# A one-core GNN and mixture-of-experts kernel: the shared expert's gate and up products between the router and the first routed expert, its down products beside the last one

## What is computed

```
# layer 3 (L3_ffn): shared expert of 768 hidden units
y_shared = jax.nn.silu(t @ Wsg.T) * (t @ Wsu.T) @ Wsd.T
y = (y_routed + y_shared).reshape(b, s, h)
```

## Time and profile before

| | us |
|---|---|
| median of 3 runs | 1854.82 (1854.15 to 1860.57) |
| the profiled execution's own time | 1854.55 |
| its span, first to last instruction | 1852.4 |
| PE busy in it | 1738.4 (94%) |
| `L0_ffn` on PE, about | 540 to 767 |
| expert part of `L3_ffn`, about | 1677 to 1848 |

### The profile page before, as it was taken

The page is one execution under the profiler, slowest core; times in us unless marked ns, Lnnn a source line. Parts: engine busy times, 40 slices in busy tenths (PEclk is TensorE's granted clock), DMA queues, the critical chain, the costliest instruction groups (busy, mean ns, idle before and its releaser), DMA issues.

```text
span 1852.4 us, 27529 instructions
## 1 busy us (share of the span) xinstructions
PE 1738.4 (94%) x12224; PEld 1040.0 (56%) x12224; DVE 624.6 (34%) x1179; ACT 444.2 (24%) x816; POOL 26.7 (1%) x35
## 2 busy tenths in 40 slices
PE   7999899998999999889999988887999999999999
PEld 4675445764456555667654433334575645766566
DVE  4415795038972221361321000002422322234320
ACT  0014684047841110251210000002411010131110
POOL 0000000000000000000000000000002000000000
PEclk9999899999999999989999999999999899999999
DMA  9315875238646877402579999999362154204660
GB/s 375 113 33 188 212 218 207 93 125 220 213 172 239 324 307 284 161 1 103 205 282 389 428 429 429 428 427 428 149 268 102 67 231 194 113 26 153 232 231 18
DMA packets 80749, 408.28 MB, mean 220 GB/s; under 512 B 9768, under 2 KB 50240, under 8 KB 58992
## 3 DMA queue, kind: packets, MB, share of 16 engines
q1 hardware_dynamic: 76112, 402.41, 57.0%
q10 hardware_dynamic: 4512, 4.03, 0.7%
HBM read 400.85 MB, written 5.51 MB: 219 GB/s over the span
## 4 chain that ended last, share of the span: by engine, by line
PE 81%; DMA 12%; DVE 5%; issue 1%; ACT 1%; SPq 0%; POOL 0%; DVEq 0%; ACTq 0%
PE banks L114 79%; DMA weight_ring<-in_L_ffn_c_fc_dram 6%; PE banks L117 2%; DMA weight_ring<-in_L_ffn_c_proj_e_dram 2%; DMA weight_ring<-in_L_gnn_W_in_dram 2%; DVE weight_ring L120 1%; DMA gate_queries<-in_L_gnn_query_rep_dram 1%; DVE stat L266 1%; DVE xn_tok L125 0%; DMA query_parts<-gate_query_parts 0%; DMA ident<-in_c_ident_dram 0%; DVE xT L137 0%; ACT weight_ring L148 0%; DMA node_parts<-gate_node_parts 0%; DVE rgat_xr L137 0%
## 5 line engine op out<-in xcount | busy, mean ns | idle before, releaser
L114 PE MATMUL banks<-weight_ring,xT 128*128 128x384 f32 x864 | 293.5, 492 | 1.5 <-DVE rgat_xr L137 1.5
L120 DVE TENSOR_TENSOR weight_ring<-weight_ring,gate_queries 128x1024 f32<-128x1024 f32 x192 | 223.7, 1221 | 31.6 <-DMA gate_queries<-in_L_gnn_query_rep_dram 15.8
L114 PEld LDWEIGHTS banks<-weight_ring,xT 128*128 128x128 f32 x864 | 162.7, 192 | 109.0 <-issue 8.8
L148 ACT ACTIVATE weight_ring<-banks 128x1024 f32<-128x1024 f32 x192 | 191.0, 1024 | 57.8 <-PE banks L114 54.7
L114 PE MATMUL banks<-xT,weight_ring 128*128 128x256 f32 x792 | 178.7, 380 | 3.2 <-ACT x_tok L151 3.2
L114 PEld LDWEIGHTS banks<-xT,weight_ring 128*128 128x128 f32 x792 | 149.7, 190 | 29.0 <-issue 5.1
L114 PE MATMUL banks<-weight_ring,r_xd 128*32 128x384 f32 (+1 forms) x2304 | 142.7, 406 | 1.1 <-DVE r_xd L124 0.6
L114 PE MATMUL banks<-weight_ring,moe_xdT 128*64 128x384 f32 x720 | 122.0, 489 | 20.6 <-DMA weight_ring<-in_L_ffn_c_fc_dram 19.6
L114 PE MATMUL banks<-weight_ring,selrow 128*32 128x256 f32 x1536 | 104.5, 392 | 12.5 <-DVE weight_ring L120 12.4
L114 PEld LDWEIGHTS banks<-weight_ring,r_xd 128*32 128x32 f32 x2304 | 76.7, 110 | 64.2 <-issue 54.5
L114 PE MATMUL banks<-gate_rows,selrow 96*128 96x512 bf16 x384 | 109.2, 387 | 2.9 <-ACT weight_ring L148 2.2
(11 more groups left out here) (370 smaller groups left out, 1841.8 us busy)
## 6 DMA issues: line engine op xcount, KB each, us to landing
weight_ring<-in_L_ffn_c_fc_dram SPq DMA_DIRECT2D x30, 2304.0 KB, 22.4
weight_ring<-in_L_ffn_c_proj_e_dram SPq DMA_DIRECT2D x21, 2304.0 KB, 28.8
gate_queries<-in_L_gnn_query_rep_dram SPq DMA_DIRECT2D x48, 512.0 KB, 3.9
weight_slot_heads<-in_L_ffn_c_proj_e_dram SPq DMA_DIRECT2D x9, 2304.0 KB, 28.3
weight_ring<-in_L_ffn_w_gate_dram SPq DMA_DIRECT2D x8, 2304.0 KB, 10.0
weight_ring<-in_L_ffn_w_up_dram SPq DMA_DIRECT2D x8, 2304.0 KB, 9.0
weight_ring<-in_L_ffn_w_down_dram SPq DMA_DIRECT2D x8, 2304.0 KB, 9.2
weight_ring<-in_L_ffn_w_dram SPq DMA_DIRECT2D x16, 1152.0 KB, 7.6
```

The source lines that it names most:

```text
L114: return self.e.matmul(out, lhsT, rhs, start=start, stop=stop)
L120: return self.e.tensor_tensor(out, a, b, op)
L148: return self.e.activation(out, a, f, **kw)
```

## The change

In both steps the shared expert's gate and up products move ahead of the first routed expert, and its down products, cut in three, take their places in the two hooks and in `combine_last_pe`; `shared_pe` is gone. In layer 0 the alpha row is spread behind the chunks, and the multiplication of the hidden units with alpha is one DVE instruction over all three chunks during expert 1. The slots, the alpha row and the shared chunks use other PSUM banks than before, with waits where a bank is used again. The shared gate and up weights are loaded ahead of the first routed expert's, so that in layer 0 the first load inside the GNN step is now two DMAs of 1152 KB in place of one of 2304 KB.

```diff
         def packed_pe(pe, B):
             s, hc = B["stage"], B["hc"]
-            pair_dispatch_pe(pe, B, 0, (0, 1, 2))
+            key = B["shared"][0]
+            shared_gate_pe(pe, B["shared"], 0)
+            slots_pe(pe, "L0_ffn", B["sc"][1], 4)
+            shared_up_pe(pe, B["shared"], 0)
+            pair_dispatch_pe(pe, B, 0, (0, 1))
+            shared_gate_pe(pe, B["shared"], 1)
+            pair_dispatch_pe(pe, B, 0, (2,))
+            shared_up_pe(pe, B["shared"], 1)
+            pe.wait_ge(*at("shared_h", (key, 0)))
+            shared_gate_pe(pe, B["shared"], 2)
+            pe.wait_ge(*at("shared_h", (key, 1)))
+            rows_to_all_pe(pe, "L0_ffn", B["gt"][:, :, NEXP:NEXP + 1], 1)
+            shared_up_pe(pe, B["shared"], 2)
+            pe.wait_ge(*at("xd_act", (s, 0, 1)))
             weights_turn(pe, B, 0)
+            spread_pe(pe, "L0_ffn", alpha_row)
...
         def both_experts_pe(pe, B):
-            s, hc = B["stage"], B["hc"]
+            s, hc, key = B["stage"], B["hc"], B["shared"][0]
+            shared_gate_pe(pe, B["shared"], 0)
+            shared_up_pe(pe, B["shared"], 0)
             pair_dispatch_pe(pe, B, 0, (0, 1, 2))
+            for o in range(1, DC):
+                if o == 2:
+                    pe.wait_ge(*at("xd_dve", (s, 0, 0)))
+                elif o == 3:
+                    pe.wait_ge(*at("xd_act", (s, 0, 1)))
+                else:
+                    pe.wait_ge(*at("shared_h", (key, {1: 0, 4: 1, 5: 2}[o])))
+                shared_gate_pe(pe, B["shared"], o)
+                shared_up_pe(pe, B["shared"], o)
+            pe.wait_ge(*at("shared_h", (key, 3)))
             weights_turn(pe, B, 0)
...
         def combine_last_pe(pe, B):
-            shared_gate_pe(pe, B["shared"], 1)
-            shared_up_pe(pe, B["shared"], 1)
+            shared_down_pe(pe, B["shared"], 2)
             combine_A(pe, B, NEXP // 2 - 1, (0, 1))
-            combine_B(pe, B, NEXP // 4 - 1)
+            combine_B(pe, B, NEXP // 4 - 1, True).then_inc(*mark("unit_free", B["shared"][4]))
...
+        def shared_down_pe(pe, shared, third):
+
+            key, hc, gate_u, up_u, down_u, h, tmp = shared
             dw = w3(unit(down_u, 0, hc * D), hc, D)
             pe.wait_ge(*loaded(down_u))
-            for o in range(hc):
-                pe.wait_ge(*at("shared_h", (key, o)))
+            pe.wait_ge(*at("shared_h", (key, "scaled") if hc < DC else (key, hc - 1)))
+            for o in range(third * hc // 3, (third + 1) * hc // 3):
...
-            load(q, ("L0g", 0), dram["L0_ffn_w_gate"][0])
-            gate_loop_sp(q, 1, (("L0u", 0), dram["L0_ffn_w_up"][0]))
+            load(q, "L0s", dram["L0_ffn_ws_gate"], dram["L0_ffn_ws_up"])
+            gate_loop_sp(q, 1, (("L0g", 0), dram["L0_ffn_w_gate"][0]))
```

More of the change, by code:

```diff
@@ L366, in rows_to_all_dve, with spread_pe, spread_dve @@
             v.wait_ge(*at("columns", key))
-            v.cp(tmp[0:n, :], PS[0:n, 4, 0:T]).then_inc(*mark("row_sb", key))
-        def spread_pe(pe, key, rows, n):
+            v.cp(tmp[0:n, :], PS[0:n, 5, 0:T]).then_inc(*mark("row_sb", key))
+        def spread_pe(pe, key, row):
             pe.wait_ge(*at("row_sb", key))
[L371 to L381, removed]
+            pe.mm(PS[:, 5, 0:T], selrow[0:1, 0, :], row[0:1, :], True, True).then_inc(*mark("spread", key))
+        def spread_dve(v, key, dst):
+            v.wait_ge(*at("spread", key))
+            v.cp(dst, PS[:, 5, 0:T]).then_inc(*mark("spread_dve", key))
         def first_max(v, oh, s, top, tmp):
@@ L421, in logits_of, with slots_pe @@
             return PS[:, bank, 0:32].rearrange("p (c n) -> p c n", c=TC)[:, :, 0:n]
-        def slots_pe(pe, key, mask):
+        def slots_pe(pe, key, mask, bank=5):
             pe.wait_ge(*at("mask", key))
@@ L1247, in beside_silu_pe @@
             if e == NEXP - 1:
[L1248 to L1252, removed]
+                shared_down_pe(pe, B["shared"], 0)
             elif e % 2:
@@ L1365, in first_pair_dve @@
             weigh_dve(v, B, 1)
+            shared_dve(v, B["shared"], 0)
             pair_xd(v, B, 0, 0, "dve")
@@ L1371, in packed_dve @@
             first_pair_dve(v, B)
+            shared_dve(v, B["shared"], 1)
+            rows_to_all_dve(v, "L0_ffn", alpha_row, 1)
+            shared_dve(v, B["shared"], 2)
+            spread_dve(v, "L0_ffn", alphas[:, 0, :])
             for e in range(NEXP):
@@ L1433, in packed_act @@
             s, silu = B["stage"], B["silu"]
+            shared_act(a, B["shared"], 0)
             pair_xd(a, B, 0, 1, "act")
+            for o in range(1, B["shared"][1]):
+                shared_act(a, B["shared"], o)
             cb_copy(a, B, 0)
@@ L1469, in both_pe @@
             if e == 0:
-                pe.wait_ge(*at("cbT", (s, 0)))
+                pe.wait_ge(*at("shared_h", (B["shared"][0], 4)))
             for k in range(DC):
@@ L1513, in both_dve @@
             first_pair_dve(v, B)
+            for o in range(1, DC):
+                shared_dve(v, B["shared"], o)
             for e in range(NEXP):
@@ L1598, in shared_dve @@
[L1598 to L1605, removed]
+                        pe.mm(PS[:, 2 * c + hf, 0:HALF], h[:, o, c * P:(c + 1) * P],
+                              dw[:, o, hf * HALF:(hf + 1) * HALF], False, False)
@@ new lines, in shared_act, with shared_dve @@
+        def shared_act(a, shared, o):
+            key, hc, gate_u, (ukey, u0), down_u, h, tmp = shared
+            if o >= 4:
+                a.wait_ge(*at("shared_h", (key, o - 4)))
+            a.wait_ge(*(at("shared_up", (key, o)) if o < hc - 1 else at("unit_free", ukey)))
+            a.act(tmp[:, o % 4, :], PS[:, shared_bank(hc, o), 0:T], ACT.Silu).then_inc(*mark("shared_silu", (key, o)))
+        def shared_dve(v, shared, o):
+            key, hc, gate_u, up_u, down_u, h, tmp = shared
+            v.wait_ge(*at("shared_silu", (key, o)))
+            v.tt(h[:, o, :], PS[:, shared_bank(hc, o), T:2 * T], tmp[:, o % 4, :],
+                 ALU.mult).then_inc(*mark("shared_h", (key, o)))
```

85 lines of the change are left out of this document (33 added, 52 removed).

## The result

The changed kernel takes 1843.56 us in the median of 8 executions (1842.15 to 1848.14), beside 1857.64 for the kernel before in its own 8 (1854.15 to 1863.21): ratio 0.9924, 95% interval 0.9910 to 0.9938. That is 14.1 us less, with 11.5 to 16.7 by the interval. The forecast was 8.25 us less.

What follows compares the result with a forecast made beforehand. It took PE to bound the kernel for most of the span (81% of the chain). Layer 0 -6.25, layer 3 -2.1 and first load +0.1 gave -8.25 us from 1854.82, so 1846.6 us; range 1843.8 to 1850.2.

Steps and rivals of the forecast that it cites:

- no measurable change: Whole kernel: a time within about 0.5%, 9.3 us, of before; chance 0.62, against 0.36 faster and 0.02 slower.
- rival E: Whole kernel: the freed end or fewer slow stretches later give more, over 10 us: 1843.5 us; chance 0.04.
- the first load: GNN step before layer 0's experts: SP issues one more DMA ahead of the first query load; bounds 0 and 0.44, taken +0.1.
- The waits are gone: Fronts of both layers' experts: PE's idle of 3.57 us in layer 0 and 1.42 + 0.62 in layer 3 is covered.
- The clock in layer 0's dispatch: Dispatch of 24 records at layer 0's front: 4.00 us at clock 1.00 instead of 6.45, about 2.3 us gained.
- The clock elsewhere: Layer 3's front: clock already 1.00, dispatch priced at 4.00 us; net -2.1 us there, just the two idle rows.
- rival B: Both fronts: only the waits are gained, the slow stretch being chance or turning up elsewhere: about -5.2, 1849.6 us; chance 0.13.
- C: Both steps: a new wait, for instance DVE's list held by the silu, loses half the gain: about -4, 1850.8; chance 0.06.
- D: Load ring: expert 1's up weights land late and PE stands; slower, 1864 us at a landing of 42 us; chance 0.02.
- fewer slow stretches: Later in the kernel: one of rival E's two grounds for a gain over 10 us.
- The freed end: Ends from which shared work is taken: rival E's other ground for a gain over 10 us.
- the prediction's own signs: Wrong if dispatch stays at 0.50, PE waits on `shared_h` or weights, second GNN loop is >0.5 us later, or untouched stages change.

Runs made afterwards that it cites:

- experiment 4: Kernel before, with six never-read idle products in PE's waits at the front of layer 0's experts: 1849.67 us, ratio 0.9948.
- experiment 5: Kernel before, unchanged, timed against itself under its own label: 1857.81 us, ratio 0.9999.
- experiment 6: Changed kernel with expert 0's gate load (one DMA of 2304 KB) first and the shared pair behind it: 1845.6 us, ratio 0.9942 to the kernel before.
- experiment 10: Changed kernel with twelve idle products that never execute, in L0_ffn's jumped-over overflow block: 1837.31 us, ratio 0.9905 to the kernel before.
- experiments 7 and 12: Changed kernel with twelve (7) or four (12) executed idle products before layer 0's expert 4: 1842.43 us (7), 1840.56 us (12).
- experiment 3: Kernel before, with only layer 0's first gate load split into two DMAs of 1152 KB: 1856.9 us, ratio 0.9987.
- experiment 9: Kernel before with twelve idle products that never execute, in L0_ffn's jumped-over overflow block: 1851.19 us, ratio 0.9969.

## Why the prediction was wrong

Forecast was 1846.6 us and no measurable change with 0.62; the kernel took 1843.56, just outside the range of 1843.8 to 1850.2, and it is faster by 0.76%. The range was to take most of rival E, but E's own price, 1843.5, lay outside it, and the result stands there. The mechanism was right. Two terms of the sum were mis-sized: the first load, set at +0.1 and about -1.0 by the traces, and the clock, priced from one execution and in one place only (1.0 us). With 0.4 us by which the front of layer 0 is shorter than its sum they make 2.5 us of the 4.75 that are missing; the rest is open. By its own steps:

**The waits are gone: right.** 3.57 us in layer 0 and 2.04 in layer 3 are away, and no new wait came. The front of `L0_ffn` was to last 21.84 us from the residual's end, and is 567.88 - 546.55 = 21.33. From the start of the residual it grew from 16.96 to 25.85, so expert 0 starts 8.89 us later against 9.40 forecast, and that half microsecond is the difference between -6.25 and -6.66 and a little more.

**The clock in layer 0's dispatch: right.** The 24 dispatch records now take 2.76 + 1.46 less 0.3 of tails at clock 1.00, and experiment 4 gained the same by idle products alone. The Trainium skill's warning ("TensorE: Matmul & The Clock Gate", "What's actually happening"), that such slow products can differ from run to run, was the other value. It did not hold for this place in the kernel before, whose front is 16.96 to 17.04 us long in all six profiles that have it untouched.

**The clock elsewhere: put at nothing, from one profile.** The warning does hold in layer 3, where two executions of the kernel before have the dispatch at 4.17 and at 5.85 us (experiment 5). In the old order a fast residual is lost again in the dispatch. In the new order nothing behind the residual is slow, so a fast residual is kept. The prediction priced layer 3's dispatch from the execution that had it fast. It named layer 0's slow residual only under rival B, priced no other outcome of it, and it dismissed play between executions because two times of three lay 0.67 apart; the third was 6 us above them.

The same shows in layer 0. The residual ahead of the front took 4.4 to 5.2 us in all seven profiles with the old order; with the new one it did so in five, and in two (experiments 6 and 10) it ran at clock 1.00:

```profile
540.90 2.83 PE L114 MATMUL banks<-x_tok,ident 128*128 128x384 f32 x8
```

There `L0_ffn` takes 210.92 us instead of 212.24, and `L3_ffn` 166.25 (experiment 10) instead of 168.08. Over the profiles with the new order the means are 211.8 (five, without those of experiments 7 and 12, which lengthen the step) and 167.5 (seven), that is -7.1 and -2.7. One profile of the changed kernel shows -8.8, the means -9.8.

**The price of the first load: the step that failed in its sign.** I took "+0.1", from bounds of nothing and 0.44, on the ground that the bytes ahead of the query load stay the same. The bytes do, but they come as two loads of 1152 KB, and behind two of these the query load lands in 8.57 to 9.79 us (seven profiles, mean 9.21), behind one of 2304 KB in 10.18 to 11.01 (seven, mean 10.63). In the changed kernel's chain:

```profile
408.22 9.48 DMA gate_queries<-in_L_gnn_query_rep_dram
```

These lengths differ by 1.4 us in the mean, but the query load is issued about 0.5 us later (0.96 us after the first weight load's issue in the changed kernel, 0.49 in the earlier trace rows). From the start of the last group of issues ahead of the weights (`gate_rows<-node_parts` x8 on SP) to the landing it is 16.92 us behind one load and 15.95 behind two, in the mean of the same seven profiles each: a net gain of 1.0 +- 0.3. So the added issue does count, as the prediction's upper bound had it, and the earlier landing outweighs it. In time the edit alone is worth 1.4 +- 0.9 us in the kernel before (experiment 3), and taking it back costs the changed kernel 1.7 +- 1.7 (experiment 6); neither is clear of noise. The bounds excluded a gain with no reason but the byte count. Why two loads of half the size let the next one land sooner is not shown.

**The size from one profile.** The sum was made against an execution of 1854.55 and a median of three, 1854.82. With 76 executions the mean is 1857.5: both were on the fast side, by 3 us. Had I started from 1857.5, the same terms would have given 1849.3, further from the result. Taken as a difference, the forecast of 8.25 stands against 13.0 +- 1.1.

Rivals B, C and D did not occur: the clock came, and neither a new wait nor a late ring did (with the shared pair loaded first, no wait for a DMA stands in PE's list from the start of `L0_ffn` to its end). In size it was rival E, over 10 us, which had 0.04. Of its grounds, fewer slow stretches carries 1.0 us by the profiles. The freed end carries none that they show: from the gap to the first products of the attention the next stage takes 58.0 +- 0.6 us in the mean of the seven profiles with `L0_ffn` in the old order, and 59.5 +- 0.3 in the seven in the new one.

**What adds up.** Steps over several profiles 9.8, the first load 1.0: 10.8 of 13.0 +- 1.1, and 9.3 if the 1.5 us that the next stage is longer belong to the change. The recorded clock says the same in another way. The part of the time that it was under full, time x (1 - clock), is 39.1 us in the kernel before (0.9789) and 33.3 in the changed one (0.9819): 5.8 us less, where the dispatch term had 2.3. The rest fell by 7.2, where the forecast's other terms had 5.95 and the load's gain adds some 1.0. This is bookkeeping, since the clock is also low while PE waits (0.72 from 768.0 to 773.8, in the gap of the kernel before). Between executions the time goes with the mean clock, by 1.4 us for each 0.001 in the kernel before and 1.5 in the changed one; at the mean clock of the kernel before, the line through the changed kernel's 15 executions gives 1848.9, a gain of 8.6. The other 4.4 come with the higher clock, of which the slow stretches named above are a part. What stays open is 2.2 to 3.7 us, two to three times the error, and which stages hold it: the lengths of single profiles scatter by as much. By the prediction's own signs it was wrong in that time was found in stages that the diff doesn't touch.

**The gap is no part of the miss.** It stands in both kernels. It does mean that an edit to PE's program ahead of `L1_gnn` can win or lose 6 to 7 us by position alone, and experiment 4 would have been misread without it: of the 10.0 us in its mean (1847.5 +- 1.7), 2.5 are clock and the rest is about what experiment 9 gets from the gap alone.

## What to carry to other kernels

Work that PE must do anyway is best put where PE waits on another engine's short chain: it closes the waits, here 5.6 us in two steps, and it keeps the granted clock up for the products behind, here 2.3 us in one dispatch. Price it over several profiles, since one can show a slow stretch in another place than the next, and try both sides of a transfer's cost: here the same bytes in two loads let a load behind them land 1.0 us sooner, the added issue counted. Before crediting an edit with microseconds in a stage that it doesn't touch, put the same number of instructions where they never execute; here this alone was worth 6.8 us, and with the change it makes the fastest version (1837.31 us). In the view of DMAs, packets of the kind "instruction" tell where to look.

## What was not expected of the hardware

- Twelve products in a block that is jumped over made the kernels 6.8 +- 1.0 and 6.9 +- 2.7 us faster; the gap they remove stands behind that block, one group of four records after PE resumes, and ends 1.2 to 1.5 us after a 16 KB packet of an instruction queue. Four executed products ahead of it do too. Where the limit lies was not tried.
- From its own issue, a 512 KB load lands 1.4 us sooner behind two loads of 1152 KB than behind one of 2304 KB, and the ranges of seven profiles each don't overlap; with the added issue 1.0 us is left.
- Eight 128x384 records of the residual take 4.52 us at clock 0.61 and 2.83 at 1.00, and the kernel before shows both in its layer 3. In the old order the step is the same length either way, because the dispatch behind is slow instead (5.85 us, not 4.17).
- The alpha multiply, three of 0.424 us in the forecast, is one instruction of 0.951 us over 128x768.
